# Normalising the feed-forward's layer norm on ScalarE instead of VectorE, with the bias made on GpSimd

## The reference

```python
h = shift_token(x); q, k, v = split(h @ wqkv)          # 8 heads of 64
q, k = rotary_xpos(l2norm(q) * qs, l2norm(k) * ksc)
x = x + local_attention(q, k, v) @ wo                  # windows of 64, one window back
h = shift_token(x)
mu = h.mean(-1); var = h.var(-1)
h = (h - mu) / jnp.sqrt(var + 1e-05) * lg + lb         # the norm that the change is about
a, g = split(h @ w1 + b1)                              # 2 x 341 columns
x = x + (a * gelu(g)) @ w2 + b2
```

## Time and profile before

| | |
|---|---|
| three executions | 469.17, 470.61, 472.55 us |
| the profiled execution, its time | 471.67 us |
| its span, first to last instruction | 469.9 us |
| busy: PE, DVE, POOL, ACT | 359.3, 329.7, 298.2, 285.0 us |
| mean granted TensorE clock | 0.916 of full speed |
| chain that ended last, by engine | PE 38%, DVE 22%, POOL 17%, issue 10%, ACT 7% |

### The profile page before, as it was taken

How to read it: one execution, slowest core, us unless ns; L and a number is a source line. 1 busy time by engine, 2 the same in 40 slices (tenths; PEclk the granted TensorE clock), 3 DMA queues, 4 the chain that set the end, 5 groups by cost and what they waited for, 6 DMA issues and landing times.

```text
span 469.9 us, 11254 instructions
## 1 busy us (share of the span) xinstructions
PE 359.3 (76%) x3832; PEld 295.0 (63%) x3832; DVE 329.7 (70%) x744; ACT 285.0 (61%) x852; POOL 298.2 (63%) x248
## 2 busy tenths in 40 slices
PE   2573057898788998899899989998949896768362
PEld 1352036777676877687778767876838775656342
DVE  6879864678668768867877796768767866743423
ACT  3453075777676777777867867767827773664020
POOL 2200348999999499949975994899477958520212
PEclk9996575999999999999999999999979999797857
DMA  8500230511431052115113320431015201200100
GB/s 274 174 0 0 53 110 19 125 30 30 108 79 31 1 146 61 28 29 152 30 30 105 79 58 1 130 79 31 12 38 130 55 1 28 64 12 1 23 22 22
DMA packets 42399, 28.21 MB, mean 60 GB/s; under 512 B 21700, under 2 KB 36598, under 8 KB 42358
## 3 DMA queue, kind: packets, MB, share of 16 engines
q1 hardware_dynamic: 42357, 27.68, 22.7%
HBM read 13.51 MB, written 3.15 MB: 35 GB/s over the span
## 4 chain that ended last, share of the span: by engine, by line
PE 38%; DVE 22%; POOL 17%; issue 10%; ACT 7%; DMA 3%; SPq 2%; DVEq 1%; POOLq 0%; ACTq 0%
POOL rn L483 6%; PE bank L717 5%; DVE h L1083 4%; PE bank L682 4%; PE bank L554 4%; DVE rot_sin L1059 4%; PE bank L550 4%; PE upper L666 3%; PE bank L551 3%; DVE rot_cos L1059 3%; POOL rot L519 3%; ACT probs L833 2%; POOL rot L504 2%; PE bank L610 2%; POOL rot L505 2%
## 5 line engine op out<-in xcount | busy, mean ns | idle before, releaser
L833 ACT ACTIVATE probs<-upper,neg_max 128x128 f32<-128x128 f32 x256 | 90.4, 369 | 62.6 <-DVE neg_max L1105 62.6
L483 POOL TENSOR_TENSOR rn<-floored,minus_half 128x16 f32<-128x16 f32 x32 | 93.8, 2930 | 2.7
L504 POOL TENSOR_TENSOR rot<-rot_cos,rot_sin 128x512 f32<-128x512 f32 x32 | 40.9, 1278 | 64.9 <-DVE rot_sin L1059 47.1
L1105 DVE TENSOR_REDUCE neg_max<-upper 128x4 f32<-128x512 f32 x64 | 43.1, 683 | 34.4 <-PE upper L666 34.4
L519 POOL TENSOR_TENSOR rot<-rot,rn 128x1024 f32<-128x1024 f32 x32 | 60.9, 1903 | 1.9
L550 PE MATMUL bank<-wqkv_hi,act_t_hi 128*128 128x512 f32 x96 | 44.2, 460 | 21.4 <-DVE o_tok L1117 13.3
L833 ACT ACTIVATION_READ_ACCUMULATOR probs<-upper,neg_max 128x1 f32 x256 | 52.9, 207 | 0.0
L1059 DVE TENSOR_TENSOR rot_cos<-bank,tab 128x512 f32<-128x512 f32 x64 | 43.6, 682 | 2.7 <-PE bank L554 2.2
L1059 DVE TENSOR_TENSOR rot_sin<-bank,tab 128x512 f32<-128x512 f32 x64 | 43.5, 680 | 0.0
L1066 DVE TENSOR_REDUCE ss<-sq 128x16 f32<-128x1024 f32 x32 | 38.8, 1212 | 5.2 <-ACT sq L854 5.1
L550 PEld LDWEIGHTS bank<-wqkv_hi,act_t_hi 128*128 128x128 f32 x96 | 19.0, 198 | 36.0 <-issue 23.3
(11 more groups left out here) (129 smaller groups left out, 883.1 us busy)
## 6 DMA issues: line engine op xcount, KB each, us to landing
v_mid<-v_tok SPq DMA_DIRECT2D x64, 128.0 KB, 2.3
tab_raw<-tables SPq DMA_DIRECT2D x8, 512.0 KB, 3.3
h_tok<-group_in SPq DMA_DIRECT2D x14, 128.0 KB, 3.4
x_res<-group_in SPq DMA_DIRECT2D x28, 64.0 KB, 1.8
wqkv_raw<-wqkv SPq DMA_DIRECT2D x2, 768.0 KB, 6.7
x_in<-x SPq DMA_DIRECT2D x4, 256.0 KB, 3.4
head_scale<-head_scales SPq DMA_DIRECT2D x8, 128.0 KB, 3.9
group_in<-normed SPq DMA_DIRECT2D x4, 256.0 KB
```

Source lines behind the costliest of these rows:

```text
L483: pool.tensor_tensor(rn[:, 0:2 * HEADS], floored[:, 0:2 * HEADS], minus_half[:, :], ALU.pow).then_inc(rn_ready, 1)
L504: pool.tensor_tensor(rot[cur.par][:, :, 0:32], rot_cos[:, :, 0:32], rot_sin[:, :, 32:64], ALU.add).then_inc(rot_added, 1)
L833: last = act.activation(probs[:, h, :], s_bank[half][:, (h % 4) * P:(h % 4 + 1) * P], ACT.Exp, bias=neg_max[a.par][:, h:h + 1], accum_out= ...
```

## The change

The four DVE instructions at j = 2 are taken out. ACT gets four instructions in the same step, between its copy of the probabilities and its copy of q; they compute `scale * h2 + bias` in place, with the row's reciprocal deviation as scale and `-mean * reciprocal deviation` as bias. POOL makes that bias at j = 1 with two more instructions of four columns, one before `deviation_roots` and one after it; `deviation_roots` signals the new semaphore `h2_root`, for which POOL waits before the second, and that second one signals `h2_dev`. The outer norm of `y_out` stays on DVE.

```diff
+        h2_mean, h2_shift = sb("h2_mean", [P, GT]), sb("h2_shift", [P, GT])
...
+        h2_means, h2_root = sem("h2_means"), sem("h2_root")
...
                     if j == 1 and not (number and G < 1):
-                        deviation_roots(G, h2_var, h2_floored, h2_dev)
+                        pool.wait_ge(h2_var, G)
+                        need(pool, h2_ready, G - 1)
+                        settle(pool)
+                        pool.tensor_scalar(h2_mean[:, :], mean_var[:, 0:GT, 0], -1.0, None, ALU.mult).then_inc(h2_means, 1)
+                        deviation_roots(G, h2_var, h2_floored, h2_root)
+                        pool.wait_ge(h2_root, G)
+                        pool.wait_ge(h2_means, G)
+                        pool.tensor_tensor(h2_shift[:, :], h2_mean[:, :], rn[:, 2 * HEADS:], ALU.mult).then_inc(h2_dev, 1)
...
+                    if j == 2 and not (number and G < 1):
+                        act.wait_ge(h2_dev, G)
+                        for k in range(GT):
+                            last = act.activation(h2[:, k, :], h2[:, k, :], ACT.Identity, bias=h2_shift[:, k:k + 1],
+                                                  scale=rn[:, 2 * HEADS + k:2 * HEADS + k + 1])
+                        last.then_inc(h2_ready, 1)
...
-                    if ffn:
-                        normalise_tiles(h2, h2, h2_dev, G).then_inc(h2_ready, 1)
```

## The result

The change made the kernel slower by about 0.4%: the median of 14 runs is 473.09 us, that of 14 runs of the kernel before is 471.85 us (the three shown ahead of the prediction are among them). The ratio of the two is 1.0038, with a 95% interval of 1.002 to 1.0056, which on 470.61 us is +0.9 to +2.6 us. The prediction was +1.4 us, a median of 472.0; the median after lies 1.1 us above that, as the 14 runs of the kernel before lie 1.24 us above the median of the three. By the two medians the change costs 1.24 us, by the ratio 1.8. The profiled execution after took 473.07 us, with a span of 471.3 us and a mean granted TensorE clock of 0.923.

A forecast was written before the change was run, and what follows sets the result against it. PE's transposes of h2 were taken as bound by DVE's path, with POOL's 0.38 us behind and last after the change. 6 x 0.07 + 0 + 0.98 = +1.4 us on 470.61 gives 472.0 us, range 468.7 to 475.0.

The forecast's parts named there:

- The two meeting paths: At PE's transposes of h2, DVE's path and POOL's path meet; DVE's is only 0.38 us longer, in G = 2.
- The forecast's own sign: PE's transposes of h2 (L689) stay within 0.1 us of 3.97 us after L1090's start.
- POOL's two instructions: POOL at j = 1: L519 0.45 us later, net +0.07 us a pass, bounds -0.04 to +0.30.
- DVE's relief: Removing four DVE instructions frees 3.2 us in six passes; DVE gains nothing that PE sees.
- ACT's four instructions: ACT at j = 2: normalising takes about 1.64 us, costs nothing, covered by PE's products with the values.
- the prediction's other estimate, 1.17: ACT's four instructions at 1.17 us, from the skill's 350 cycles per copy; G = 8 would lose 0.5 us instead.
- Rival C: ACT beside POOL's sums is stretched like DVE, four instructions taking 3.2 us: +7.9 us, 478.5 us; chance 6%.
- The last pass: G = 8, every step on the path: bias 0.45 us later, ACT 0.53 more, +0.98 us, bounds +0.8 to +1.3.
- A: POOL's additions are hidden and PE's wait for h2 goes: -1.2 us, 469.4 us; chance 10%.
- B: DVE's relief carries on, POOL's 0.72 us waits for the sum of squares become time: -5.5 us, 465.1; chance 4%.

The follow-up runs named there:

- first experiment: POOL's two small instructions for the bias added to the kernel before, DVE still normalising h2 and the bias unused; ratio 1.0071 to the kernel before, +3.3 us.
- fifth experiment: Kernel before, with only the deviation roots of h2 moved behind POOL's multiplication of rot at j = 1; ratio 1.0229, +10.8 us.
- second experiment: Changed kernel, but one DVE instruction at j = 2 makes the bias and POOL's queue is as before the change; ratio 0.9968 to the kernel before, -1.5 us.
- The third: Kernel before, with POOL's rotary sums at j = 2 waiting until DVE has normalised h2; ratio 0.9922, -3.7 us.
- fourth: Changed kernel, with all of POOL's work for h2 put behind its multiplication of rot at j = 1; ratio 1.0102 to the kernel before, +4.8 us.

## Why the prediction was right, and where it was not

**The two meeting paths.** The reading that carried the forecast, 0.38 us between DVE's and POOL's path and not 19 us in a chain, held for the change: the wait went away and the growth of the other took its place. The forecast's own sign, transposes within 0.1 us of 3.97 after the mark, was missed: they came at 4.15.

**POOL's two instructions.** Forecast +0.45 us, measured 0.59 on POOL and 0.62 in PE's wait. The mis-sized piece is the guard ahead of the first one, 0.12 us, which the prediction put at nothing. The net per pass is +0.18 instead of +0.07, inside the bounds that the prediction gave (-0.04 to +0.30).

**DVE's relief costs nothing and gives nothing.** Right: 3.2 us a pass became 3.35 us more of waiting.

**ACT's four instructions.** Forecast 1.64 us, measured 1.65 (the prediction's other estimate, 1.17, is not borne out); no stretch beside POOL. Rival C is refuted. The Trainium skill's rule that ScalarE does not wait for the shared ports (SBUF — State Buffer, Who interferes with whom) agrees with the 1.65 or 1.66 us of all eight groups, six beside POOL and two not.

**The last pass.** Forecast +0.98. From POOL's first small instruction on it is +1.03, but the whole pass lost 1.41 us, more than the upper bound of +1.3: the guard stands here too (0.15), and DVE's means took 0.24 us longer for a reason that is open. That the forecast +1.4 us lies within the measured +0.9 to +2.6 although both terms of its sum were too small is in part luck: the trace gives +2.5.

**Rivals A and B.** A would have had the transposes more than 0.3 us earlier relative to the mark; they came 0.18 later. B needed POOL's L481 to matter; its wait of 0.72 us went away, but POOL's queue ahead of it was later by nearly as much, 0.63 us, and it starts 5.14 us after the mark, before 5.15.

**What the prediction had wrong without its sum showing it.** It took DVE's 3.22 us as a duration and DVE's path as independent of POOL's. The first and the fifth experiment show otherwise: the normalisation ends with the fourth POOL instruction that overlaps it, in each of the six passes of the kernel before and of both experiments. Had it stayed on DVE, POOL's two instructions would have cost 0.60 us a pass (1.0071) and not 0.18. Measured by its own parts the change is thus a gain and a loss: moving the norm to ACT gives back about half of what making its bias on POOL costs. The second experiment, 0.9968 with the bias elsewhere, shows the same from the other side.

**Open.** The first experiment's ratio, +3.3 us, is explained by 0.57 to 0.61 us in each of six passes, 3.5, and about 0.4 in the last. The third's, -3.7, is larger than the 2.3 us that its trace shows, though its interval (-5.1 to -2.2) holds them. In the fourth and fifth, what the distances don't explain lies mostly in stretches with a lower granted clock; why it was lower was read and not tested. Whether fewer and larger DVE instructions (over all four tiles at once, with mean and root spread along the columns) would meet fewer of POOL's was not tried.

## What to carry to other kernels

When the chain names an engine, look at what PE waited for one step earlier: here 0.38 us separated the named path from the next, and the next one ran through the very queue that the change made longer. An instruction that takes three times as long in one pass as in another is not slow but shut out; find which engine's instruction each piece ends with, and hold that one back, before moving the work. An edit that loses 2.3% alone and one that wins 0.8% alone were worth 1.9% together, because each frees one of two paths that meet.

## What the runs showed of the hardware that was not expected

Four `tensor_scalar` instructions of 128x128 on DVE, float32 in SBUF, beside a run of GpSimd instructions, got in one at each end of a GpSimd instruction, each ending 0.08 to 0.09 us behind it (once 0.12): 3.22 us in four slots, 3.83 with a longer first slot, 3.52 in another order. With GpSimd waiting they took 1.11 to 1.28 us (1.57 once, where the first slot was 0.3 us longer). GpSimd's own sums took 1.25 to 1.31 us with DVE's instructions beside them and without. The exception is the pass G = 3 of the kernel before and of the first experiment, where a GpSimd memset went ahead of a DVE instruction that was already waiting, and two of DVE's then ended 0.06 us apart.

The Trainium skill (SBUF — State Buffer, Who interferes with whom) says, of VectorE's two-port modes, that whoever issues first holds the shared ports for a whole instruction and the other blocks. The traces agree; which mode DVE was in no row shows. What these runs add is the order: with the memset as the exception, GpSimd's next instruction did not get ahead of a waiting DVE, and DVE's next did not get ahead of GpSimd.
